# Scores of the rotary cross-attention: plain fp32 products, or three rounded products of high and low parts

## The chip, the cores and the metric

The kernel runs on one core of a Trainium2 chip. Its metric is the device time of one execution in microseconds (us); lower is better. Engines are called by their names in the profile: PE is TensorE (PEld its loads of the stationary operand), DVE is VectorE, ACT is ScalarE, POOL is GpSimd, SP issues the transfers.

## The reference

Six residual blocks on x (2 batches, 128 tokens, 512 wide). The change lies in the first, a cross-attention of 16 heads of 64 over a context of 2 x 2048 rows:

```python
lat = layer_norm(latents, ln_lat_g, ln_lat_b)          # 2 x 128 x 512
ctx = layer_norm(context, ln_ctx_g, ln_ctx_b)          # 2 x 2048 x 512
q = (lat @ Wq).reshape(b, n, HEADS, DHEAD).transpose(0, 2, 1, 3)
k, v = jnp.split(ctx @ Wkv, 2, axis=-1)                # 16 heads of 64
k = apply_rope(k, cos[None, None], sin[None, None])    # rotary, keys only
attn = jnp.einsum('bhnd,bhsd->bhns', q, k) * DHEAD ** (-0.5)
attn = jax.nn.softmax(jnp.clip(attn, -11.0, 11.0), axis=-1)
out = jnp.einsum('bhns,bhsd->bhnd', attn, v)
return out.transpose(0, 2, 1, 3).reshape(b, n, INNER) @ Wo + bo
```

Behind it come a causal self-attention, a product with the signs of a weight, a second cross-attention, a second causal self-attention and a mixture of experts. Everything is fp32.

## The kernel before

The first stage is `cross_attention_rotary`. The 4096 context rows are worked on in 8 chunks of 512 (`NC = 8`), four to a batch; the 16 heads in 4 groups of 4. A round t (`NT = 32`) is one chunk n = t // 4 with one group g = t % 4. A head's 64 components are two halves of 32 (the rotary pairs), and the four heads of a group lie on the four row groups of 32 partitions.

The engines run their own instruction streams in the written order and meet at semaphores. In a round:

- PE: in even rounds `values(v)` (L618, the value projection of half a chunk, four banks of `u_ps`) and `transposes` (L598) of half the next chunk; then `project(t)` (L633, the keys of chunk and group into the two banks of `k_ps`), `scores(t - 1)` (L648), `weigh(t - 2)` (L672). Projections are `split_matmul` (L55 to L59): each operand is split into a high part, rounded to the type fp32r, and a low part, the rounded rest; the product is high x high + high x low + low x high, each one matmul on rounded operands.
- `scores` is not split: for each of 4 column blocks j, 2 halves a and 4 heads i there is one plain fp32 product (L667) of a stationary 32 x 128 block of `turned` (rotated keys) with 128 columns of `q_T` (queries), and head i goes to bank i of `u_ps`.
- DVE: `turn(t)` (L331) rotates the keys out of `k_ps` into `turned` with six operations of 512 columns; `clip(t - 1)` (L354); and for chunk n + 2, spread over the rounds g = 1, 2 and 3, `stats`, `spread` and `center` (its layer norm, in place in `ctx_raw`). In round 18 it also takes two long reciprocals (L413), in round 19 it normalises the first batch (L419), in round 28 it adds the output bias.
- ACT: in even rounds `values` (copies of the values) and `context` (two writes a transposed quarter, one full, one rounded); `exponent(t - 1)`; `root`, the square root for a chunk's layer norm, in round g = 2.
- POOL: `split` makes the context's low part; `add_up(t - 1)` sums the probabilities, behind `clip`.
- SP: context (`ctx_raw`) and rotary tables (`tabs`) have two buffers each and are loaded a chunk or more ahead; then the output weights and those of the next stage.

The lowest 64 KB of the placed memory (`place`) hold the split weights of values and keys; the next stage's weights are loaded over them. The waits around the change, in `scores` and in `project`:

```python
pe.wait_ge(s["rope"], 6 * t + 6)                     # scores(t): rotation of round t complete
pe.wait_ge(s["exped"], 4 * t)                        # and the exponentials of round t - 1
...
pe.wait_ge(s["rope"], 6 * (t - 1) + 2 * a + 2)       # project(t): bank a of k_ps has been read
```

Of the kernel before, what the change touches and what calls it, by code (L numbers as in the profile page):

```python
# [16 lines left out]
ALU = mybir.AluOpType  # L17
# [139 lines left out]
def cross_attention_rotary(nc, I, env):  # L157
# [12 lines left out]
    with ExitStack() as st:  # L170
        names = ("vecs_in", "wq_in0", "wq_in1", "ctx_in0", "ctx_in1", "tab_in0", "tab_in1",
# [3 lines left out]
                 "wv_hi", "wv_lo", "wk_hi", "wk_lo", "v_mm", "v_out", "k_mm", "rope", "score", "exped", "clipped",  # L175
# [3 lines left out]
        s_ctx = [s["ctx_in0"], s["ctx_in1"]]  # L179
        s_tab = [s["tab_in0"], s["tab_in1"]]  # L180
# [16 lines left out]
        den = sb_in(st, "den", [P, 2, 512])  # L197
        bo = sb_in(st, "bo", [P, D])
# [17 lines left out]
        wo = ctx_raw[:].rearrange("p a c d -> p (a c) d")  # L216
# [11 lines left out]
        def _(sp):  # L228
            def load_ctx(n):
                if n >= 2:  # L230
                    sp.wait_ge(s["ctp"], 4 * (n - 1))
                sp.dma_start(ctx_raw[:, n % 2, :, :], I["ctx_rows"][n * 512:(n + 1) * 512, :]
                             .rearrange("(c p) d -> p c d", p=P)).then_inc(s_ctx[n % 2], 16)

            def load_tab(n):
                if n >= 2:
                    sp.wait_ge(s["rope"], 24 * (n - 1))
                c = n % 4
                sp.dma_start(tabs[:, n % 2, :, :], I["rot_tabs"][c * P:(c + 1) * P, :]
                             .rearrange("p (a n) -> p a n", a=2)).then_inc(s_tab[n % 2], 16)  # L240
# [21 lines left out]
            load_ctx(1)  # L262
# [5 lines left out]
            load_tab(1)  # L268
            load_wk(2)
            load_wk(3)  # L270
            load_ctx(2)
            for n in range(2, NC):
                if n + 1 < NC:
                    load_ctx(n + 1)
                load_tab(n)
                if n == 3:
                    sp.dma_start(env["causal"][:], I["causal4"]).then_inc(env["small_in"], 16)
                    for name, t in env["mo_small"].items():
                        sp.dma_start(t[:], I[name]).then_inc(env["small_in"], 16)
            rows4 = lambda n: I[n].rearrange("(k p) n -> p k n", p=P)  # L280
            sp.dma_start(bo[:], I["bo0"]).then_inc(s["bo_in"], 16)
            sp.wait_ge(s["ctp"], 4 * NC)
            sp.dma_start(wo, rows4("wo0")).then_inc(s["wo_in"], 16)
# [8 lines left out]
        def stats(dve, n):  # L292

            dve.wait_ge(s_ctx[n % 2], 16 * (n // 2 + 1))
            for c in range(4):
                dve.bn_stats(cst[:, c, :], ctx_raw[:, n % 2, c, :]).then_inc(s["c_step"], 1)
# [8 lines left out]
        def center(dve, n):  # L305
# [3 lines left out]
            for c in range(4):  # L309
                dve.tensor_scalar(ctx_raw[:, n % 2, c, :], ctx_raw[:, n % 2, c, :], cmv[:, n % 2, c, 0:1],  # L310
                                  crs[:, n % 2, c:c + 1], ALU.subtract, ALU.mult).then_inc(s["c_step"], 1)
# [6 lines left out]
        def _(dve):  # L318
# [12 lines left out]
            def turn(t):  # L331

                n, r = t // 4, t % 2
                cos, sin = tabs[:, n % 2, 0, :], tabs[:, n % 2, 1, :]
                if t % 4 == 0:
                    dve.wait_ge(s_tab[n % 2], 16 * (n // 2 + 1))
# [6 lines left out]
                if t >= 1:  # L343
# [8 lines left out]
                                  ALU.add).then_inc(s["rope"], 1)  # L352

# [26 lines left out]
            center(dve, 0)  # L380
            low_v(0)
            low_v(1)
            stats(dve, 1)
# [6 lines left out]
            for t in range(NT + 1):  # L390
                n, g = t // 4, t % 4
                if t < NT:
                    turn(t)
                if t >= 1:
                    clip(t - 1)
                if t == 1:
                    low_k(2)
                    low_k(3)
                if t < NT and 2 <= n + 2 < NC:
                    if g == 1:  # L400
                        stats(dve, n + 2)
# [8 lines left out]
                if t == 18:  # L410
                    dve.wait_ge(s["den_out"], 2)
                    for u in range(2):
                        dve.reciprocal(den[:, u, :], den[:, u, :]).then_inc(s["recip"], 1)  # L413
                if t == 19:
                    for u in range(2):
# [3 lines left out]
                        dve.tensor_tensor(half, half, den[:, u, :].rearrange("p (a t) -> p a t", a=4),  # L419
                                          ALU.mult).then_inc(s["normalised"], 1)  # L420
            for k in range(8):
# [4 lines left out]
                dve.reciprocal(den[:, k // 4, cols], u_ps[:, 2 + k // 4, cols]).then_inc(s["recip"], 1)  # L426
                dve.wait_ge(s["recip"], 2 + k + 1)
                dve.tensor_tensor(attn_T[:, k, P:2 * P], o_ps[:, k // 4, cols], den[:, k // 4, cols],
# [18 lines left out]
        def _(act):  # L447
# [1616 lines left out]
```

## Time and profile before

| | |
|---|---|
| time, median of 3 runs | 1193.22 us (1191.4 to 1197.19) |
| the profiled execution's own time | 1196.15 us |
| its span, first to last instruction | 1194.4 us |
| mean granted TensorE clock | 0.994 |
| TensorE busy | 1174.4 us, 98% |
| VectorE / ScalarE / GpSimd busy | 688.8 / 540.1 / 217.0 us |

The rotary stage ends some 541 us into the span; its 32 bursts of scores lie between 50.3 and 520.4. A row of the profile names engine, line, operation, the tile written and those read. "32\*128 32x128" is the stationary shape, then the moving one. A "busy" sum counts overlapping instructions once, so a mean duration times a count can be far more than it. Durations of matmuls include their way through the array; what one costs a stream is the distance between starts. A time in brackets at the end of a row is idle time before it, and what ended it.

### The profile page before, as it was taken

The page shows a single profiled execution, that of the slowest core. Times are in us where ns is not written, and L with a number is a line of the kernel's source. Part 1 is how long each engine was busy: PE and PEld are TensorE (multiplying, and loading weights), DVE is VectorE, ACT ScalarE, POOL GpSimd, SP SyncE. Part 2 cuts the span into 40 slices and gives each one's busy share as a digit, 9 for nine tenths or more (in the row PEclk, how much of TensorE's full clock was granted, in tenths as well). Part 3 has the DMA queues.
Part 4 walks back from the last instruction along what each step waited for, and adds up shares of the span by engine and source line. Part 5 has one row for each costly group of instructions (what it writes and reads, how often), then busy time and mean ns, then how long its engine had stood idle before and what let it go on. Part 6 is the DMA issues. An engine that isn't in the chain of part 4 may idle for free.

```text
span 1194.4 us, 23415 instructions
## 1 busy us (share of the span) xinstructions
PE 1174.4 (98%) x9888; PEld 963.8 (81%) x9888; DVE 688.8 (58%) x1220; ACT 540.1 (45%) x907; POOL 217.0 (18%) x178
## 2 busy tenths in 40 slices
PE   8999999999999999999899999999999999999998
PEld 6888888888788888864546667888899999999997
DVE  4654554545464533466788885265765566566562
ACT  4433324332433322224359997373644544444441
POOL 2243343444333443350000000010000000000000
PEclk9999999999999999999989999999999999999999
DMA  8210201010100020245232324301545445445440
GB/s 302 71 55 1 66 2 52 4 36 19 36 19 2 27 72 1 83 139 212 96 152 79 136 108 178 142 1 72 228 159 211 161 192 211 157 195 207 158 162 19
DMA packets 28160, 126.06 MB, mean 106 GB/s; under 512 B 2715, under 2 KB 2971, under 8 KB 17572
## 3 DMA queue, kind: packets, MB, share of 16 engines
q1 hardware_dynamic: 28068, 124.74, 27.9%
q8 instruction: 69, 1.13, 0.4%
q14 instruction: 23, 0.19, 0.0%
HBM read 124.20 MB, written 0.52 MB: 104 GB/s over the span
## 4 chain that ended last, share of the span: by engine, by line
PE 49%; issue 2%; DVE 2%; ACT 2%; DVEq 0%
PE mid_bk L57 11%; PE mid_bk L58 10%; PE mid_bk L59 10%; PE mid_bk L1105 5%; PE mid_bk L1120 2%; PE mid_bk L1150 2%; PE mid_bk L1076 2%; PE mid_bk L995 2%; PE mid_bk L1140 1%; PE mid_bk L1249 0%; ACT sa_sc L1415 0%; PE mid_bk L1201 0%; PE mid_bk L1190 0%; PE mid_bk L1050 0%; PE mid_bk L986 0%
## 5 line engine op out<-in xcount | busy, mean ns | idle before, releaser
L565 POOL TENSOR_TENSOR norm_both<-norm_both,prob 128x512 f32<-128x512 f32 x118 | 155.4, 1317 | 145.6 <-DVE prob L357 138.2
L494 ACT ACTIVATE prob<-u_ps 128x512 f32<-128x512 f32 x128 | 66.2, 605 | 181.5 <-PE u_ps L667 181.5
L57 PE MATMUL mid_bk<-mo_x_hi,mo_w_hi 128*128 128x256 f32 x496 | 141.0, 284 | 0.0
L58 PE MATMUL mid_bk<-mo_x_lo,mo_w_hi 128*128 128x256 f32 x496 | 141.0, 284 | 0.0
L59 PE MATMUL mid_bk<-mo_x_hi,mo_w_lo 128*128 128x256 f32 x496 | 141.0, 284 | 0.0
L340 DVE TENSOR_TENSOR turned<-k_ps,tabs 128x512 f32<-128x512 f32 x32 | 22.1, 690 | 189.7 <-PE k_ps L59 189.6
L1788 DVE TENSOR_TENSOR mo_w_lo<-w_raw,mo_w_hi 128x2048 fp32r<-128x2048 f32 x32 | 73.3, 2292 | 72.7 <-ACT mo_w_hi L1497 72.7
L57 PE MATMUL k_ps<-ctx_hi,wk_hi 128*128 128x512 f32 x256 | 102.8, 402 | 0.0
L57 PE MATMUL u_ps<-wv_hi,ctx_hi 128*128 128x512 f32 x256 | 101.7, 397 | 0.8 <-ACT prob L494 0.8
L483 ACT ACTIVATE vals<-u_ps 128x512 f32<-128x512 f32 x64 | 38.3, 598 | 141.2 <-PE u_ps L59 141.1
L1497 ACT ACTIVATE mo_w_hi<-w_raw 128x2048 fp32r<-128x2048 f32 x32 | 61.2, 1913 | 87.9 <-PE mid_bk L59 87.9
L57 PE MATMUL mid_bk<-mo_w_hi,mo_h_hi 128*128 128x512 f32 x256 | 100.2, 391 | 0.0
L58 PE MATMUL k_ps<-ctx_lo,wk_hi 128*128 128x512 f32 x256 | 100.2, 391 | 0.0
L58 PE MATMUL u_ps<-wv_lo,ctx_hi 128*128 128x512 f32 x256 | 100.1, 391 | 0.0
L58 PE MATMUL mid_bk<-mo_w_lo,mo_h_hi 128*128 128x512 f32 x256 | 100.0, 391 | 0.0
L59 PE MATMUL u_ps<-wv_hi,ctx_lo 128*128 128x512 f32 x256 | 99.7, 389 | 0.0
L59 PE MATMUL k_ps<-ctx_hi,wk_lo 128*128 128x512 f32 x256 | 99.7, 389 | 0.0
L59 PE MATMUL mid_bk<-mo_w_hi,mo_h_lo 128*128 128x512 f32 x256 | 99.6, 389 | 0.0
L58 PEld LDWEIGHTS mid_bk<-mo_x_lo,mo_w_hi 128*128 128x128 f32 x496 | 95.9, 193 | 1.2
L57 PEld LDWEIGHTS mid_bk<-mo_x_hi,mo_w_hi 128*128 128x128 f32 x496 | 95.8, 193 | 1.2
L59 PEld LDWEIGHTS mid_bk<-mo_x_hi,mo_w_lo 128*128 128x128 f32 x496 | 95.8, 193 | 0.0
L1505 ACT ACTIVATE mo_hid<-mid_bk,mo_b_cur 128x256 f32<-128x256 f32 x128 | 53.7, 472 | 86.8 <-PE mid_bk L59 86.7
(264 smaller groups left out, 2357.2 us busy)
## 6 DMA issues: line engine op xcount, KB each, us to landing
w_raw<-in_w SPq DMA_DIRECT2D x64, 1024.0 KB, 6.3
ctx_raw<-in_ctx_rows SPq DMA_DIRECT2D x8, 1024.0 KB, 5.5
x_k<-in_ctx_T SPq DMA_DIRECT2D x8, 1024.0 KB, 7.0
x_val<-in_ctx_heads SPq DMA_DIRECT2D x8, 1024.0 KB, 5.0
tabs<-in_rot_tabs SPq DMA_DIRECT2D x8, 512.0 KB, 3.8
vals<-in_wq_rows SPq DMA_DIRECT2D x4, 512.0 KB, 7.6
ctx_raw<-in_wo SPq DMA_DIRECT2D x1, 2048.0 KB, 9.7
x_mask<-in_mask SPq DMA_DIRECT2D x2, 1024.0 KB, 9.0
```

The costliest lines, as they stand in the source:

```text
L57: pe.matmul(out, w_hi, x_hi, start=start, stop=False)
L58: pe.matmul(out, w_hi, x_lo, start=False, stop=False)
L59: return pe.matmul(out, w_lo, x_hi, start=False, stop=stop)
L483: act.activation(vals[:, i, hv * 512:(hv + 1) * 512], u_ps[:, i, :], ACT.Copy).then_inc(s["v_out"], 1)
L494: act.activation(prob[:, t % 2, i, :], u_ps[:, i, :], ACT.Exp).then_inc(s["exped"], 1)
L565: ins = pool.tensor_tensor(to, to, src, ALU.add)
L995: ins = pe.matmul(bk[b][:, m, :], normed_T[:, k, b * P:(b + 1) * P], (wq, wk, wv)[m][:, k, :], start=(m == 2 and k == 0), stop=(k == KD - 1))
L1076: pe.matmul(s_ps[:, a, :], normed_T[rows, g, b * P:(b + 1) * P], k_raw[rows, n % 2, c * 512:(c + 1) * 512], start=True, stop=True).then_in ...
L1105: ins = pe.transpose(turned_at(q, a)[:, k * P:(k + 1) * P], x_sc[:, n % 2, a, (4 * c + k) * P:(4 * c + k + 1) * P], ident[:])
L1497: act.activation(w2_hi[:, r, :, :], w2_raw[:, r, :, :], ACT.Copy).then_inc(mo["w2_hi"], 1)
L1505: act.activation(hid[:, r, n, :], h_ps[:, 2 * r + n // 2, (n % 2) * TOK:(n % 2 + 1) * TOK], ACT.Gelu_apprx_tanh, bias=b1_cur[:, r, n:n + 1 ...
L1788: dve.tensor_tensor(w2_lo[:, r, :, :], w2_raw[:, r, :, :], w2_hi[:, r, :, :], ALU.subtract).then_inc(mo["w2_lo"], 1)
```

## The change

The scores become three rounded products like those of `split_matmul`: rounded keys `t_hi` with rounded queries `q_hi`, `t_hi` with the queries' low part `q_lo`, the keys' low part `t_lo` with `q_hi`. For it ACT rounds the rotated keys in every round (`high_turned`, behind the exponentials of the round before) and DVE subtracts (`low_turned`, behind `clip`); queries are rounded by ACT and their low part taken by DVE. `t_lo` lies over `turned`, `q_lo` under `den`. To make room, context and tables have one buffer in place of two, the bias lies in `causal` until that is loaded, the output weights are in two halves, and the next stage's weights `wp` are loaded in the next block. `center` moves from round g = 3 to the head of the next chunk's first round, `stats`, `spread` and `root` to round g = 3; the bias is added in round 13 and not 28.

```diff
@@ tiles and names
-        slabs = sb_in(st, "slabs", [P, 64 * 256 + (env["floor"] - env["base"]) // 4])
+        turned, den = place("turned", [P, 2, 2, 512], 64), place("den", [P, 8, TOK], 72)
+        t_lo, q_lo = place("t_lo", [P, 2, 2, 512], 64, F32R), place("q_lo", [P, NQ, 2, TOK], 72, F32R)
+        slabs = sb_in(st, "slabs", [P, 80 * 256 + (env["floor"] - env["base"]) // 4])
...
-        ctx_raw = sb_in(st, "ctx_raw", [P, 2, 4, D])
+        ctx_raw = sb_in(st, "ctx_raw", [P, 4, D])
-        tabs = sb_in(st, "tabs", [P, 2, 2, 512])
+        tabs = sb_in(st, "tabs", [P, 2, 512])
-        q_T = sb_in(st, "q_T", [P, NQ, 2, TOK])
-        turned = sb_in(st, "turned", [P, 2, 2, 512])
+        q_hi = sb_in(st, "q_hi", [P, NQ, 2, TOK], F32R)
+        t_hi = sb_in(st, "t_hi", [P, 2, 2, 512], F32R)
...
-        bo = sb_in(st, "bo", [P, D])
+        bo = env["causal"]
...
+        wo_half = ctx_raw, place("wo_second", [P, 4, D], 24)
@@ SP
             def load_ctx(n):
-                if n >= 2:
-                    sp.wait_ge(s["ctp"], 4 * (n - 1))
+                if n >= 1:
+                    sp.wait_ge(s["ctp"], 4 * n)
...
             def load_tab(n):
-                if n >= 2:
-                    sp.wait_ge(s["rope"], 24 * (n - 1))
+                if n >= 1:
+                    sp.wait_ge(s["rope"], 24 * n)
...
             load_wv(1)
-            load_ctx(1)
             load_wk(0)
             load_tab(0)
             load_wk(1)
             load_wv(2)
             load_wv(3)
-            load_tab(1)
+            load_ctx(1)
             load_wk(2)
             load_wk(3)
...
+            for n in range(NC):
+                if n >= 1:
+                    load_tab(n)
+                if n + 2 < NC:
+                    load_ctx(n + 2)
+                if n == 1:
+                    sp.dma_start(bo[:], I["bo0"]).then_inc(s["bo_in"], 16)
...
+                if n == 5:
+                    sp.wait_ge(s["bo_added"], NB)
+                    sp.dma_start(env["causal"][:], I["causal4"]).then_inc(env["small_in"], 16)
             sp.wait_ge(s["ctp"], 4 * NC)
...
             sp.wait_ge(s["v_mm"], 4 * 2 * NC)
-            for n, w in env["sa0_w"].items():
-                sp.dma_start(w[:], rows4("sa0_" + n)).then_inc(env["sa0_w_in"], 16)
+            sp.dma_start(wo_half[1][:], I["wo0"][512:1024, :].rearrange("(k p) n -> p k n", p=P)).then_inc(s["wo_in"], 16)
+            for n in ("wq", "wk", "wv"):
+                sp.dma_start(env["sa0_w"][n][:], rows4("sa0_" + n)).then_inc(env["sa0_w_in"], 16)
@@ DVE
+            def low_turned(t):
+                dve.wait_ge(s["t_hi"], t + 1)
+                dve.tensor_tensor(t_lo[:, t % 2, :, :], turned[:, t % 2, :, :], t_hi[:, t % 2, :, :],
+                                  ALU.subtract).then_inc(s["t_lo"], 1)
+
+            def low_queries(g):
+                dve.wait_ge(s["q_hi"], g + 1)
+                dve.scalar_tensor_tensor(q_lo[:, g, :, :], k_ps[:, g % 2, :].rearrange("p (a t) -> p a t", a=2), 0.125,
+                                         q_hi[:, g, :, :], ALU.mult, ALU.subtract).then_inc(s["q_out"], 1)
...
             center(dve, 0)
+            low_queries(0)
+            low_queries(1)
             low_v(0)
             low_v(1)
+            low_queries(2)
+            low_queries(3)
             stats(dve, 1)
...
             for t in range(NT + 1):
                 n, g = t // 4, t % 4
+                if 1 <= n and n + 1 < NC and g == 0:
+                    center(dve, n + 1)
                 if t < NT:
                     turn(t)
                 if t >= 1:
                     clip(t - 1)
+                if t < NT:
+                    low_turned(t)
...
-                if t < NT and 2 <= n + 2 < NC:
-                    if g == 1:
-                        stats(dve, n + 2)
-                    elif g == 2:
-                        spread(dve, n + 2)
-                    elif g == 3:
-                        center(dve, n + 2)
-                if t == 28:
+                if n + 2 < NC and g == 3:
+                    stats(dve, n + 2)
+                    spread(dve, n + 2)
+                if t == 13:
                     dve.wait_ge(s["bo_in"], 16)
@@ ACT
             def queries(g):
                 act.wait_ge(s["q_mm"], g + 1)
-                act.activation(q_T[:, g, :, :], k_ps[:, g % 2, :].rearrange("p (a t) -> p a t", a=2), ACT.Copy,
-                               scale=0.125).then_inc(s["q_out"], 1)
+                act.activation(q_hi[:, g, :, :], k_ps[:, g % 2, :].rearrange("p (a t) -> p a t", a=2), ACT.Copy,
+                               scale=0.125).then_inc(s["q_hi"], 1)
+
+            def high_turned(t):
+                act.wait_ge(s["rope"], 6 * t + 6)
+                act.activation(t_hi[:, t % 2, :, :], turned[:, t % 2, :, :], ACT.Copy).then_inc(s["t_hi"], 1)
...
                 if t >= 1:
                     exponent(t - 1)
-                if t < NT and n + 2 < NC and g == 2:
+                if t < NT:
+                    high_turned(t)
+                if t < NT and n + 2 < NC and g == 3:
                     root(act, n + 2)
@@ PE
             def scores(t):
...
-                pe.wait_ge(s["rope"], 6 * t + 6)
+                pe.wait_ge(s["t_lo"], t + 1)
...
                 for j in range(4):
                     cols = slice(j * P, (j + 1) * P)
-                    for a in range(2):
+                    for a, m in ((0, 0), (0, 1), (0, 2), (1, 0), (1, 1), (1, 2)):
+                        part_t, part_q = ((t_hi, q_hi), (t_hi, q_lo), (t_lo, q_hi))[m]
                         for i in range(4):
                             rows = slice(32 * i, 32 * i + 32)
-                            ins = pe.matmul(u_ps[:, i, cols], turned[rows, t % 2, a, cols],
-                                            q_T[rows, g, a, b * P:(b + 1) * P], start=(a == 0), stop=(a == 1))
+                            ins = pe.matmul(u_ps[:, i, cols], part_t[rows, t % 2, a, cols],
+                                            part_q[rows, g, a, b * P:(b + 1) * P], start=(a == 0 and m == 0),
+                                            stop=(a == 1 and m == 2))
...
-            pe.wait_ge(s["wo_in"], 16)
+            pe.wait_ge(s["wo_in"], 32)
@@ next stage
+            sp.dma_start(wp[:], rows("sa0_wp")).then_inc(sa0_w_in, 16)
             for n in range(2):
                 load_keys(n)
...
             def project_values(b):
+                pe.wait_ge(sa0_w_in, 16 * 10)
...
-            dve.wait_ge(sa0_w_in, 16 * 10)
             moments(1, 1)
```

## Rows read from the trace of the kernel before

**Rows 1.** The page, busy us, share of the span and instructions.
```profile
PE 1174.4 (98%) x9888; PEld 963.8 (81%) x9888; DVE 688.8 (58%) x1220; ACT 540.1 (45%) x907; POOL 217.0 (18%) x178
```
**Rows 2.** Busy time (instructions) by stretch: PE, PEld, DVE, ACT, POOL; clock, DMA.
```profile
210.00:270.00 60.00, 60.00 (x585) 50.21 (x585) 29.78 (x52) 21.13 (x35) 24.77 (x19) 1.00 0.08 20
```
**Rows 3.** Order of time around a burst of scores: start, duration, instructions.
```profile
256.31 1.88 PEld L667 LDWEIGHTS u_ps<-q_T,turned 32*128 32x128 f32 x64 [0.35 <-issue]
258.31 1.97 PE L683 MATMUL o_ps<-prob,vals 128*64 128x128 f32 x32
...
260.20 0.19 PEld L57 LDWEIGHTS k_ps<-ctx_hi,wk_hi 128*128 128x128 f32 x1 [0.17 <-issue]
260.31 0.19 PEld L58 LDWEIGHTS k_ps<-ctx_lo,wk_hi 128*128 128x128 f32 x1
```
**Rows 4.** Groups by line in the stage: count, busy us, mean ns, idle before.
```profile
L667 PEld LDWEIGHTS u_ps<-q_T,turned 32*128 32x128 f32 x2048 | 60.1, 186 | 11.5 <-issue 11.5
L58 PEld LDWEIGHTS k_ps<-ctx_lo,wk_hi 128*128 128x128 f32 x256 | 48.1, 188 | 9.1
...
L322 DVE TENSOR_TENSOR wv_lo<-prob,wv_hi 128x1024 fp32r<-128x1024 f32 x2 | 2.4, 1222 | 9.1 <-ACT wv_hi L451 9.1
...
L451 ACT ACTIVATE wv_hi<-attn_T 128x1024 fp32r<-128x1024 f32 x2 | 2.0, 1044 | 0.0
```
**Rows 5.** Order of time, loads of the experts' routing product.
```profile
829.67 0.97 PEld L1262 LDWEIGHTS mid_bk<-mo_wr,norm_both 128*128 128x128 f32 x8
```
**Rows 6.** Order of time, rounded products of 512 and of 256 columns.
```profile
1003.90 0.39 PE L59 MATMUL mid_bk<-mo_w_hi,mo_h_lo 128*128 128x512 f32 x1
1004.13 0.28 PE L57 MATMUL mid_bk<-mo_x_hi,mo_w_hi 128*128 128x256 f32 x1
...
1004.48 0.28 PE L57 MATMUL mid_bk<-mo_x_hi,mo_w_hi 128*128 128x256 f32 x1
```
**Rows 7.** Order of time, the second half of a chunk, all engines.
```profile
177.52 2.47 DVE L296 BATCH_NORM_STATS2 cst<-ctx_raw 128x6 f32<-128x512 f32 x4
...
199.30 1.08 DVE L303 TENSOR_SCALAR cva<-cmv 128x4 f32<-128x4 f32 x1
...
203.96 2.07 PE L667 MATMUL u_ps<-q_T,turned 32*128 32x128 f32 x64
...
206.05 2.07 ACT L494 ACTIVATE prob<-u_ps 128x512 f32<-128x512 f32 x4 [4.13 <-PE u_ps L667]
...
206.68 1.90 DVE L357 TENSOR_SCALAR prob<-prob 128x512 f32<-128x512 f32 x4
...
208.65 5.60 POOL L565 TENSOR_TENSOR norm_both<-norm_both,prob 128x512 f32<-128x512 f32 x4 [4.20 <-DVE prob L357]
...
208.70 5.84 DVE L310 TENSOR_SCALAR ctx_raw<-ctx_raw,cmv,crs 128x512 f32<-128x512 f32 x4
...
218.92 1.03 PE L602 MATMUL u_ps<-ident,ctx_raw 128*128 128x128 f32 x8
```
**Rows 8.** Order of time, the last burst of the stage.
```profile
518.30 2.07 PE L667 MATMUL u_ps<-q_T,turned 32*128 32x128 f32 x64 [0.33 <-ACT prob L494]
```
**Rows 9.** Order of time, VectorE in round 18.
```profile
325.57 6.55 DVE L413 RECIPROCAL den<-den 128x512 f32<-128x512 f32 x2
```
**Rows 10.** Order of time, the start of the stage.
```profile
31.14 1.92 DVE L310 TENSOR_SCALAR ctx_raw<-ctx_raw,cmv,crs 128x512 f32<-128x512 f32 x4
...
38.40 1.03 PE L602 MATMUL u_ps<-ident,ctx_raw 128*128 128x128 f32 x8
...
46.73 0.69 DVE L351 TENSOR_TENSOR turned<-turned,part 128x512 f32<-128x512 f32 x1
...
50.26 2.07 PE L667 MATMUL u_ps<-q_T,turned 32*128 32x128 f32 x64
```
**Rows 11.** The page, transfers: KB of one, us to landing.
```profile
ctx_raw<-in_ctx_rows SPq DMA_DIRECT2D x8, 1024.0 KB, 5.5
...
tabs<-in_rot_tabs SPq DMA_DIRECT2D x8, 512.0 KB, 3.8
```

More of the change, by code:

```diff
@@ L215, in cross_attention_rotary @@
         summed = norm_both[:].rearrange("p a n -> p (a n)").rearrange("p (h t) -> p h t", h=H)
-        wo = ctx_raw[:].rearrange("p a c d -> p (a c) d")
+        den = den[:, :, 0:P]
+        wo_half = ctx_raw, place("wo_second", [P, 4, D], 24)
+        wo = lambda k: wo_half[k // 4][:, k % 4, :]
         prob_raw = prob[:].rearrange("p a i n -> p (a i n)")
@@ L267, in _ @@
             load_wv(3)
-            load_tab(1)
+            load_ctx(1)
             load_wk(2)
             load_wk(3)
[L271 to L277, printed above, removed]
+            rows4 = lambda n: I[n].rearrange("(k p) n -> p k n", p=P)
+            for n in range(NC):
[5 more added lines that the diff above has]
+                    sp.dma_start(bo[:], I["bo0"]).then_inc(s["bo_in"], 16)
                     for name, t in env["mo_small"].items():
                         sp.dma_start(t[:], I[name]).then_inc(env["small_in"], 16)
-            rows4 = lambda n: I[n].rearrange("(k p) n -> p k n", p=P)
-            sp.dma_start(bo[:], I["bo0"]).then_inc(s["bo_in"], 16)
+                if n == 5:
+                    sp.wait_ge(s["bo_added"], NB)
+                    sp.dma_start(env["causal"][:], I["causal4"]).then_inc(env["small_in"], 16)
             sp.wait_ge(s["ctp"], 4 * NC)
-            sp.dma_start(wo, rows4("wo0")).then_inc(s["wo_in"], 16)
+            sp.dma_start(wo_half[0][:], I["wo0"][0:512, :].rearrange("(k p) n -> p k n", p=P)).then_inc(s["wo_in"], 16)
             sp.wait_ge(s["v_mm"], 4 * 2 * NC)
-            for n, w in env["sa0_w"].items():
-                sp.dma_start(w[:], rows4("sa0_" + n)).then_inc(env["sa0_w_in"], 16)
+            sp.dma_start(wo_half[1][:], I["wo0"][512:1024, :].rearrange("(k p) n -> p k n", p=P)).then_inc(s["wo_in"], 16)
+            for n in ("wq", "wk", "wv"):
+                sp.dma_start(env["sa0_w"][n][:], rows4("sa0_" + n)).then_inc(env["sa0_w_in"], 16)
             sp.wait_ge(s["k_mm"], 2 * NT)
@@ L333, in turn @@
                 n, r = t // 4, t % 2
-                cos, sin = tabs[:, n % 2, 0, :], tabs[:, n % 2, 1, :]
+                cos, sin = tabs[:, 0, :], tabs[:, 1, :]
                 if t % 4 == 0:
-                    dve.wait_ge(s_tab[n % 2], 16 * (n // 2 + 1))
+                    dve.wait_ge(s["tab_in"], 16 * (n + 1))
                 if t >= 2:
@@ L412, in _ @@
                     for u in range(2):
-                        dve.reciprocal(den[:, u, :], den[:, u, :]).then_inc(s["recip"], 1)
+                        half = den[:, 4 * u:4 * u + 4, :]
+                        dve.reciprocal(half, half).then_inc(s["recip"], 1)
                 if t == 19:
@@ L418, in _ @@
                         half = attn_T[:, 4 * u:4 * u + 4, 0:P]
-                        dve.tensor_tensor(half, half, den[:, u, :].rearrange("p (a t) -> p a t", a=4),
-                                          ALU.mult).then_inc(s["normalised"], 1)
+                        dve.tensor_tensor(half, half, den[:, 4 * u:4 * u + 4, :], ALU.mult).then_inc(s["normalised"], 1)
             for k in range(8):
@@ L709, in project_out @@
                     pe.wait_ge(s["normalised"], 2 + k + 1 if b else k // 4 + 1)
-                    ins = pe.matmul(k_ps[:, b, :], attn_T[:, k, b * P:(b + 1) * P], wo[:, k, :],
+                    ins = pe.matmul(k_ps[:, b, :], attn_T[:, k, b * P:(b + 1) * P], wo(k),
                                     start=(k == 0), stop=(k == 7))
```

34 lines of the change are left out of this document (16 added, 18 removed).

## The prediction

> **What bounds the kernel now.** I read the page's busy shares first, then the busy times by stretch, then the order of time in one round of the loop. TensorE is busy 98% of the span, the next engine 58% [rows 1]. The share is an average, so the rotary stage has to be read by itself: in the stretch shown, and in each like it from 90 to 510, TensorE is busy for 60.00 of 60.00 us at a granted clock of 1.00, while VectorE works 29.78, ScalarE 21.13, GpSimd 24.77 [rows 2]. There every microsecond that TensorE gets more or less moves the end, and the other engines count only where they make it wait. One burst of scores runs from 256.31 until the weighing starts at 258.31: 2.00 us for 64 instruction pairs, 32 bursts in all, 2048 pairs [rows 3, 4]. The loop writes 4 x 2 x 4 = 32 products, so a plain fp32 product is two pairs (load and matmul), and four of them, one for each row group, run side by side: the loads last 1.88 us with 0.19 for the last one, so the 16 foursomes follow one another every (1.88 - 0.19) / 15 = 0.113 us.
>
> **The scores, on the path.** A burst now has 4 blocks x 2 halves x 3 products x 4 row groups = 96 products in place of 32. A rounded product is one pair: the loop of the keys writes 256 for each of its three lines and 256 are recorded [rows 4]. So 64 pairs become 96, 16 foursomes 24. The question is what sets the pace of a foursome, the load or the streaming of 128 columns.
> - The load. Eight products with a moving operand of only 8 columns have loads that take 0.97 us together, so (0.97 - 0.19) / 7 = 0.111 us apart [rows 5]: with next to nothing to stream, a load of 128 columns still costs 0.11. A rounded operand's load is no shorter, 188 ns against 186 of the scores, and at the start of a projection the second rounded load follows the first after 260.31 - 260.20 = 0.11 us [rows 3, 4]. The change keeps all 128 stationary columns. Also two products that share a stationary operand load it twice (L57 and L58 do), so the shared rounded keys save none.
> - The streaming. No rounded product of this trace has fewer than 256 columns. One of 512 columns takes 1004.13 - 1003.90 = 0.23 of TensorE, three of 256 take 0.35 or 0.12 each [rows 6], so 0.11 for 256 columns more and, in proportion, 0.12 - 0.055 = 0.065 for 128: below the load. The upper bound is the plain product of two pairs, 2 x 0.113 = 0.226.
> I take 0.113 for a foursome, the load, since that row has the same 32 x 128 stationary shape. The sum: 8 more foursomes x 0.113 = 0.90 us a burst, x 32 bursts = +28.9 us. From 0.108 to 0.125 (a full burst's mean, 2.00 / 16) it would be +25.0 to +38.0 (24 times the pace less 1.81, times 32).
>
> **The rounding, beside the path.** ScalarE gets one copy of 128x1024 in a round (1.05 us, as the rounding of the values' weights [rows 4]), VectorE one subtraction of that size (1.22). VectorE works half of the time [rows 2], so 1.22 in a round of some 15.5 is carried. What counts is where they stand. With S the start of a burst in round t, the rotation of round t has ended before the exponentials of t - 1 do; these start at S + 2.1 and the clip at S + 2.8 now [rows 7], 0.9 later with the longer burst; ScalarE has the copy behind its exponentials and ends it at S + 6.1, VectorE its subtraction behind the clip and ends at S + 7.4. The scores of round t come only behind the weighing (S + 4.9) and the next projection (5.7 us more): S + 10.5, so 3 us are left. Three places have no such projection, or more in front:
> - The last round. Behind the last projection come scores(30), weigh(29) and at once scores(31), which now start 0.33 us after TensorE is free, behind the exponentials (518.30) [rows 8]. Then they wait for the low part: S + 7.4 against S + 4.9, 2.5 us, less the 0.33: +2.2 us. Behind this wait stand weigh(30), the output projection and the next stage.
> - Rounds 18 and 19. VectorE's two long reciprocals (6.55 us) [rows 9] come behind the low part of round 18 and push the rotation of 19, its clip, its low part, and now also the statistics and the centering of the context chunk, which stand behind all of them. Counting from the values of round 18: reciprocals to 33.5, rotation 37.2, clip 39.1, low part 40.4, statistics and spread 44.4, square root, the normalising pair 45.7, centering 48.0; the transposes want it at 45.8. +2.2 us, once.
> - The change of chunk, six times. The statistics moved from the second round of a chunk to its last, the centering from there to the round behind, ahead of its rotation. With S in the last round: low part S + 7.4, four statistics (2.47) 9.9, aggregate 10.3, variance (1.08) 11.3, root 11.6, centering from 12.0. The transposes want it when the values are through, at S + 15.9 (now 218.92 - 203.96 = 15.0, plus 0.9). Centering has taken 5.84 us beside four additions of GpSimd and 1.92 alone [rows 7, 10]; the additions run from S + 5.6 to 11.0, so I take 1.92, done at S + 14.0: nothing, with 1.9 us in hand. ScalarE waits in its root too, with the copies of the values behind it; TensorE asks for those only at the transposes.
>
> **The rest, at nothing.** Start: q_out is now raised by VectorE, behind ScalarE's rounding; four subtractions of some 0.7 us, the last of them behind the last query product, push the second chunk's centering back by some 3.6 us, from its end at 33.1 to 36.7; the transposes come at 38.40 [rows 10]. If the cover goes it costs what is late, under 1 us. The burst of round 0 starts at 50.26; its rotation ends at 47.4, so the low part is there at 47.4 + 1.1 + 1.2 = 49.7 [rows 10]. Context and tables now have one buffer each: the next chunk's load waits for the second pair of transposes and takes 5.5 us [rows 11], wanted over 15 us later; a table (3.8 us) is loaded behind the last rotation of its chunk and wanted 17 us later. On SP's queue each stands in the order in which it is released; the bias, asked for in round 13, is issued in round 6. The second half of the output weights waits for the last values and has one round, some 20 us, for 5. The projection weights moved to the next stage put 1 MB ahead of the keys on that queue: some 5 us of transfers; the weights are wanted only behind the next attention's weighing, the keys behind the whole of it. I price them from 0 to +2.
>
> **Sum.** 28.9 + 2.2 + 2.2 = +33.3 on the profiled execution's own 1196.15 us. That execution was 2.9 above the median of the runs, 1193.22, so the forecast is 1193.2 + 33.3 = 1226.5. Its own range is 1218 to 1236 (25.0 with no stall; 38.0 with 4.4).
>
> **Rivals.**
> - Faster: a rounded load is hidden and the stream sets the pace. At 0.065 a foursome 24 take 1.56 us against 1.81 now, -0.25 x 32 = -8; at 0.053, half of the increment for 256 columns without any overhead, -17. With the stalls, +4.4, it is 1181 to 1190; it is decided below 0.070. Against it stand the rows of 188 ns and of 0.11 us between loads. The Trainium skill's page "TensorE: Matmul & The Clock Gate", section "Weight-path perf modes — Fast Weight Load (FWL) and DoubleRow", says that fast loading is on when 128 weights are loaded and their type is not FP32; if the rounded type fell under it, the load would be short and this rival right. The trace disagrees so far, 188 ns rounded and 186 plain [rows 4]. Chance 0.07.
> - A narrow rounded product streams no faster than a plain one: 0.226 a foursome, 24 x 0.226 - 1.81 = 3.61 a burst, +115.6, with the last round's wait +118: 1311. For it: the trace has none under 256 columns, so nothing excludes it. Against: 256 and 512 are in proportion. Chance 0.11. That the row groups don't run side by side at all (96 x 0.111 = 10.7 a burst, +278) gets 0.02.
> - The change of chunk is late. If the centering meets GpSimd's additions it takes 5.84, ends at S + 17.9 and TensorE waits 2.0 us six times: +12, 1238. The Trainium skill's page "SBUF — State Buffer", section "Who interferes with whom", says that a VectorE instruction with two SBUF inputs contends with a GpSimd instruction that reads SBUF; by it the new subtraction, which starts with the additions, could wait for one of them, 1.3 us more, in the last round and in the chain of the chunk. The trace has something of it: 5.84 against 1.92 for the centering. Chance 0.12.
>
> **How the numbers follow.** Forecast 0.68, late chunk 0.12, slow narrow product 0.11, hidden load 0.07, serial 0.02. The range 1214 to 1246 holds the first two, 0.80. A measurement of this kernel tells 0.5% from no change: faster needs under 1187.3, within reaches to 1199.2. The hidden load gives the first two thirds of the time: faster 0.05, same 0.03, slower 0.92.
>
> **What would show it.** Right: the loads of a burst 23 x 0.113 + 0.19 = 2.8 us long, 96 of them, 3072 in all; bursts of 2.9 us; TensorE idle before scores(31) for 2.5 us and before the transposes of round 20 only. It would be wrong if the loads of a burst stood clearly under or over 0.11 apart, or if the transposes waited at each change of chunk.

## The result, and the profile after

The changed kernel takes 1229.38 us (median of 4 runs, 1225.54 to 1229.48), the kernel before 1195.2 us beside it (4 runs, 1191.4 to 1197.31). The ratio is 1.029, 95% interval 1.0269 to 1.0311, so the change makes the kernel slower by 34.2 us. The profiled executions have spans of 1227.5 and 1194.4 us; this difference, 33.1, is what the rows below have to account for.

The page after (busy us, share, instructions), against [rows 1]: TensorE has 1024 instructions more, the 32 more of each of 32 bursts, and its share is the same 98%.
```profile
PE 1203.5 (98%) x10912; PEld 995.0 (81%) x10912; DVE 728.1 (59%) x1256; ACT 568.4 (46%) x939; POOL 241.8 (20%) x178
```
The same dense stretch after, against [rows 2] (PE, PEld, DVE, ACT, POOL, then clock and DMA). TensorE is still busy for all 60 us at full clock; VectorE has 34.49 in place of 29.78 and is far from its limit.
```profile
210.00:270.00 60.00, 60.00 (x686) 51.00 (x686) 34.49 (x55) 22.40 (x36) 26.75 (x19) 1.00 0.09 28
```
The loads of one burst of scores in order of time (start, duration), against the load row of [rows 3]. The operands change with each foursome, so each has its own row. From 211.57 to 214.14 there are 23 steps, 2.57 us: 0.112 us each, whichever parts are multiplied. The weighing follows at 214.40: 2.83 us for the burst where it was 2.00.
```profile
211.57 0.19 PEld L692 LDWEIGHTS u_ps<-q_hi,t_hi 32*128 32x128 f32 x4 [0.35 <-issue]
211.68 0.19 PEld L692 LDWEIGHTS u_ps<-q_lo,t_hi 32*128 32x128 f32 x4
211.79 0.20 PEld L692 LDWEIGHTS u_ps<-q_hi,t_lo 32*128 32x128 f32 x4
...
214.14 0.20 PEld L692 LDWEIGHTS u_ps<-q_hi,t_lo 32*128 32x128 f32 x4
214.40 1.73 PEld L709 LDWEIGHTS o_ps<-prob,vals 128*64 128x64 f32 x32
```
TensorE's waits from 0 to 560 us (us in total, times, longest). Two are new: 3.1 us on the low part of the turned keys, once, and 1.1 us on the centering, once. The six changes of chunk don't stand there.
```profile
PE u_ps L692 <- DVE t_lo L359: 3.1, 1, 3.1
...
PE u_ps L626 <- DVE ctx_raw L313: 1.1, 1, 1.1
```
The last round of the stage on TensorE, against [rows 8]: after the weighing of chunk 29 it waits 3.14 us, then the burst begins at the usual 0.11 a foursome, and from 547.57 on each takes 0.21. The burst lasts 552.20 - 547.13 = 5.07 us and the weighing behind it 2.96.
```profile
542.03 1.97 PE L709 MATMUL o_ps<-prob,vals 128*64 128x128 f32 x32
547.13 0.33 PE L692 MATMUL u_ps<-q_hi,t_hi 32*128 32x128 f32 x4 [3.14 <-DVE t_lo L359]
547.30 0.28 PE L692 MATMUL u_ps<-q_lo,t_hi 32*128 32x128 f32 x4
547.41 0.38 PE L692 MATMUL u_ps<-q_hi,t_lo 32*128 32x128 f32 x4
547.57 0.43 PE L692 MATMUL u_ps<-q_hi,t_hi 32*128 32x128 f32 x4
547.78 0.43 PE L692 MATMUL u_ps<-q_lo,t_hi 32*128 32x128 f32 x4
...
552.20 2.96 PE L709 MATMUL o_ps<-prob,vals 128*64 128x128 f32 x32
555.09 3.70 PE L736 MATMUL k_ps<-ctx_raw,attn_T 128*128 128x512 f32 x8
```
The same place by stretch (the column behind POOL's count is the granted clock): TensorE did nothing for 3.1 us, and behind that its granted clock is 0.53, which is the lower of its two levels, 1.2 GHz, for nearly all of 7.2 us.
```profile
544.00:547.10 3.10, 0.00 (x0) 0.00 (x0) 2.50 (x3) 1.13 (x2) 2.29 (x2) 1.00 0.97 355
547.10:554.30 7.20, 7.17 (x116) 7.05 (x118) 1.26 (x3) 2.02 (x4) 3.66 (x3) 0.53 0.06 23
```
**The account of the profiled pair.** The span from the weighing of chunk 29 to the first output projection is a ruler that needs no other part of the trace: 522.19 - 516.00 = 6.19 us before, 555.09 - 542.03 = 13.06 after, +6.87. Of it 0.83 is the longer burst, 2.81 the wait (3.14 less 0.33), and 3.23 is burst and weighing at the lower clock (5.07 - 2.83, and 2.89 - 1.90 from start to start). The rows of before for it:
```profile
516.00 1.97 PE L683 MATMUL o_ps<-prob,vals 128*64 128x128 f32 x32
...
520.30 1.97 PE L683 MATMUL o_ps<-prob,vals 128*64 128x128 f32 x32
522.19 1.12 PE L710 MATMUL k_ps<-ctx_raw,attn_T 128*128 128x512 f32 x2
```
Over the stage: 32 bursts x 0.83 = +26.6, the last wait +2.8, the clock behind it +3.2, the wait in round 20 +1.1, and a start that is 0.6 us earlier. That is +33.1 against 555.09 - 522.19 = +32.9 measured. The earlier start is not the change's doing: the first transposes begin at 38.40 us before, at 37.80 here, and at 38.48 in a second profile of the changed kernel (changed_again below). Behind the stage nothing more is lost: both executions have falls of the clock there, 13.6 and 13.7 us in sum at the lower level.

### The profile page after: what moved, and what is told of

Its sections match the earlier page's. It is cut to its first block, busy times and chain, and to the rows that moved or that the text cites. A ratio compares the mean times of both kernels' runs of the same rounds, so it can differ in the third digit from the quotient of the medians.

```text
span 1227.5 us, 25534 instructions
## 1 busy us (share of the span) xinstructions
PE 1203.5 (98%) x10912; PEld 995.0 (81%) x10912; DVE 728.1 (59%) x1256; ACT 568.4 (46%) x939; POOL 241.8 (20%) x178
## 4 chain that ended last, share of the span: by engine, by line
PE 47%; DVE 2%; issue 2%; ACT 1%; DVEq 0%
PE mid_bk L57 10%; PE mid_bk L58 10%; PE mid_bk L59 10%; PE mid_bk L1133 4%; PE mid_bk L1178 2%; PE mid_bk L1148 2%; PE mid_bk L1104 2%; PE mid_bk L1022 2%; PE mid_bk L1168 1%; PE mid_bk L1277 0%; ACT sa_sc L1443 0%; DVE x_sc L1724 0%; PE mid_bk L1229 0%; PE mid_bk L1218 0%; PE mid_bk L1078 0%
## 5 line engine op out<-in xcount | busy, mean ns | idle before, releaser
L589 POOL TENSOR_TENSOR norm_both<-norm_both,prob 128x512 f32<-128x512 f32 x118 | 180.2, 1527 | 156.6 <-DVE prob L370 149.2
L1533 ACT ACTIVATE mo_hid<-mid_bk,mo_b_cur 128x256 f32<-128x256 f32 x128 | 53.6, 471 | 86.7 <-PE mid_bk L59 86.7
L1724 DVE CUSTOM_DVE_ANT_0 x_sc<-mid_bk,x_mask 128x512 f32<-128x512 f32 x128 | 80.9, 687 | 4.6 <-issue 4.6
```

Source lines behind the costliest of these rows:

```text
L589: ins = pool.tensor_tensor(to, to, src, ALU.add)
L1533: act.activation(hid[:, r, n, :], h_ps[:, 2 * r + n // 2, (n % 2) * TOK:(n % 2 + 1) * TOK], ACT.Gelu_apprx_tanh, bias=b1_cur[:, r, n:n + 1 ...
L1724: dve.tensor_tensor_reduce(x_sc[:, n % 2, a, cols], s_ps[:, a, :], mask[:, b, cols], 1.0, -3.0e38, ALU.add, ALU.max, x_tops[:, n % 2, a, c ...
```

## The experiments

Nine kernels ran. The first four and the next four each ran together beside the kernel before (medians 1193.2 and 1192.49 us), the last alone (1192.12). "First output projection" is the start of that line in a profile; the kernel before has it at 522.19 us, the changed one at 555.09. The theory: a foursome (the four products that run side by side, one for each row group) costs what its stationary load costs, 0.11 us for 128 columns, and the rest of the loss sits in the two waits and what they set off. The rivals: the matmul or its streaming sets the pace, or the frame (one buffer each, the moved order) costs much more than its waits.

**narrow_moving.** The two products with a low part move 64 columns in place of 128. In this and the next edits the stop flag and the signal at the end of the burst move to the product that is now last (not shown). The scores of half the queries so lack the correction.
```
-  for a, m in ((0, 0), (0, 1), (0, 2), (1, 0), (1, 1), (1, 2)):
+  for a, m in ((0, 0), (0, 1), (0, 2), (1, 1), (1, 2), (1, 0)):
+      w = P if m == 0 else P // 2
...
-          ins = pe.matmul(u_ps[:, i, cols], part_t[rows, t % 2, a, cols], part_q[rows, g, a, b * P:(b + 1) * P], ...)
+          ins = pe.matmul(u_ps[:, i, j * P:j * P + w], part_t[rows, t % 2, a, cols], part_q[rows, g, a, b * P:b * P + w], ...)
```


> Leaves out half of the query columns in four of the six products of each block (high x low and low x high, but for the last product, which keeps all 128): 16 of the 24 foursomes of a burst have a moving operand of 64 columns instead of 128; the loads of the stationary operand stay at 128 columns. Load theory: the loads set the pace, so nothing moves: foursomes 0.112 us apart, a burst 2.8 us to the weighing, the time within 1 us of the changed kernel's. Stream theory (a rounded product of 128 columns streams at half the rate of a wide one, 0.107 us, and the load is covered): 16 x 0.053 = 0.85 us less a burst, 2.0 us, 27 us less in all.

Measured: 1231.55 us (1229.24 to 1233.86, 2 runs), ratio 1.0319 [1.0289, 1.0349]. Foursomes with 64 moving columns start 0.11 us apart as before (402.56, 402.67), and the burst is 405.14 - 402.31 = 2.83 us, as with 128 columns:
```profile
402.31 0.33 PE L693 MATMUL u_ps<-q_hi,t_hi 32*128 32x128 f32 x4
402.48 0.25 PE L693 MATMUL u_ps<-q_lo,t_hi 32*128 32x64 f32 x4
402.56 0.28 PE L693 MATMUL u_ps<-q_hi,t_lo 32*128 32x64 f32 x4
402.67 0.28 PE L693 MATMUL u_ps<-q_lo,t_hi 32*128 32x64 f32 x4
...
405.14 3.51 PE L710 MATMUL o_ps<-prob,vals 128*64 128x128 f32 x32
```
The streaming doesn't set the pace. The clock of this kernel, and the long weighing in the last row, are taken up in the last section.

**short_load.** The mirror of it: the stationary operand of the same sixteen foursomes has 64 columns, the moving one 128. The scores of half the keys so lack the correction.
```
-  for a, m in ((0, 0), (0, 1), (0, 2), (1, 0), (1, 1), (1, 2)):
+  for a, m in ((0, 0), (0, 1), (0, 2), (1, 1), (1, 2), (1, 0)):
+      w = P if m == 0 else P // 2
...
-          ins = pe.matmul(u_ps[:, i, cols], part_t[rows, t % 2, a, cols], ...)
+          ins = pe.matmul(u_ps[0:w, i, cols], part_t[rows, t % 2, a, j * P:j * P + w], ...)
```


> The counterpart: in the same 16 foursomes of a burst the stationary operand has 64 columns instead of 128 and the moving one keeps its 128, so half of the key rows get no low-part products. Load theory: the 16 shorter loads cost about 0.055 to 0.065 us instead of 0.112, a burst takes 8 x 0.112 + 16 x 0.06 + 0.15 = 2.0 us, about 27 us less in all than the changed kernel. Stream theory: nothing moves, 2.8 us.

Measured: 1202.3 us (1198.83 to 1203.61, 3 runs), ratio 1.0067 [1.0045, 1.009]. The loads of a burst: behind a foursome of 128 columns the next starts 0.11 us later, behind one of 64 only 0.06, and 24 foursomes take 258.44 - 256.44 = 2.00 us. In a row of loads the second shape is that of the loaded, stationary operand; the products of the 64-column loads still move 128 columns.
```profile
256.44 0.19 PEld L693 LDWEIGHTS u_ps<-q_hi,t_hi 32*128 32x128 f32 x4 [0.35 <-issue]
256.55 0.14 PEld L693 LDWEIGHTS u_ps<-q_lo,t_hi 32*64 32x64 f32 x4
256.61 0.14 PEld L693 LDWEIGHTS u_ps<-q_hi,t_lo 32*64 32x64 f32 x4
...
258.44 1.73 PEld L710 LDWEIGHTS o_ps<-prob,vals 128*64 128x64 f32 x32
```
The two kernels have the same count of products and of instructions. Halving what is loaded takes 0.83 us out of a burst, halving what is streamed takes nothing: the load sets the pace. Fewer stationary columns also mean fewer rows of output, which this edit alone doesn't separate from the load; the routing product of [rows 5], with 8 moving columns and loads 0.111 us apart, speaks for the load. Since here 128 columns stream within 0.06, a load that took no time would have made the changed burst shorter than before (an estimate: 24 x 0.06 + 0.26 = 1.70 us). So the rival of the hidden load had its price about right and its condition wrong.

**plain_in_new_frame.** Everything of the change but the products: the parts are read as plain fp32 and multiplied by the two plain products of before (high parts only).
```
-  for a, m in ((0, 0), (0, 1), (0, 2), (1, 0), (1, 1), (1, 2)):
+  for a in range(2):
-          ins = pe.matmul(u_ps[:, i, cols], part_t[rows, t % 2, a, cols], part_q[rows, g, a, b * P:(b + 1) * P], ...)
+          ins = pe.matmul(u_ps[:, i, cols], t_hi[rows, t % 2, a, cols].bitcast(F32), q_hi[rows, g, a, b * P:(b + 1) * P].bitcast(F32), ...)
```


> Everything of the change but its products: buffers, order, rounding on ScalarE, subtraction on VectorE and all waits stay, the scores are again 32 plain fp32 products a burst, of the rounded keys with the rounded queries (the low parts are computed and not used). Mine: bursts of 2.0 us as before; what is left is the frame: the wait before scores(31) of about 3 us, half the clock behind it (3 us more), about 1 to 2 us before the transposes of round 20, less 0.6 at the start: 5 to 8 us above the kernel before, 1200 to 1203. Rival, that the frame costs nothing and the whole difference is the products: within 1 us of the kernel before. Rival, that the frame is the larger part: over 15 us above.

Measured: 1202.48 us (1199.64 to 1206.12, 6 runs), ratio 1.0074 [1.0052, 1.0095]: +9.3 us by the medians, a little over the 5 to 8 expected. The burst is 2.00 us again, the first output projection 529.75, +7.56. Its waits, from the list of TensorE's waits, and the last burst and weighing:
```profile
PE u_ps L691 <- DVE t_lo L359: 3.1, 1, 3.1
...
PE u_ps L626 <- DVE ctx_raw L313: 1.9, 1, 1.9
```
```profile
523.06 3.80 PE L691 MATMUL u_ps<-q_hi,t_hi 32*128 32x128 f32 x64 [3.12 <-DVE t_lo L359]
526.79 3.03 PE L707 MATMUL o_ps<-prob,vals 128*64 128x128 f32 x32
```
There are 2.8 us more in the last round, 1.9 in round 20, and 2.8 at the lower clock behind the last wait (burst 3.73 in place of 2.00, weighing 2.96 in place of 1.90 from start to start) make 7.5 of the 7.56. So the frame costs its two waits and the clock, and the other moves (single buffers, the later centering, the queue) cost nothing that shows. With shorter bursts the wait of round 20 is 1.9 and with the changed ones 1.1: the 0.83 us more of each burst cover part of it.

**two_products.** The product with the low part of the turned keys is left out: sixteen foursomes.
```
-  for a, m in ((0, 0), (0, 1), (0, 2), (1, 0), (1, 1), (1, 2)):
+  for a, m in ((0, 0), (0, 1), (1, 0), (1, 1)):
```


> Leaves out the product of the keys' low part with the rounded queries: 16 foursomes a burst instead of 24. Load theory: 2.83 - 8 x 0.112 = 1.94 us a burst, so 28 to 29 us less than the changed kernel, 1200 to 1202, still above the kernel before for the frame's waits. If a rounded foursome cost more at the start or end of a burst than inside, the burst would end clearly above 1.94.

Measured: 1201.55 us (1199.31 to 1202.78, 4 runs), ratio 1.0064 [1.0042, 1.0086], first output projection 526.55; burst 516.00 - 514.06 = 1.94 us. Sixteen rounded foursomes cost what sixteen of plain products do, less 0.06. A plain fp32 product here is just two loads of 128 columns, and three rounded ones are three.

**changed_again, fill_last_wait, weigh_first, weigh_first_late_recip.** The second set takes the last round apart. changed_again is the changed kernel once more.

> The changed kernel once more, beside the next three on the same chip. 33 to 35 us above the kernel before; 3 to 4 us less in a run in which the clock does not fall behind the wait of the last round.

Measured: 1226.87 us (1226.16 to 1230.44, 5 runs), ratio 1.0293 [1.0276, 1.031]. The last round repeats: the wait 3.14, from weighing to output projection 555.07 - 542.76 = 12.31 us. The lower clock again lasts 6.8 us, but it begins later, so part of its cost falls on the output projection (4.47 us where the changed kernel has 3.70).

fill_last_wait gives TensorE three products of no use during the wait:
```
   if t == NT:
+      pe.wait_ge(s["rope"], 6 * NT)
+      for _ in range(3):
+          pe.matmul(k_ps[:, 1, :], part[:, 0, 0:P], part[:, 1, :], start=True, stop=True)
```


> The changed kernel with three plain products of 512 columns on data that nobody needs, into a bank of k_ps that is free, between weigh(29) and scores(31): TensorE has some 2.6 us of work in the wait of 3.1 us, the wait itself stays. If the fall of the clock behind that wait costs what it seems to (a burst of 5.07 us instead of 2.83 and a weighing of 2.9 instead of 1.97), the granted clock stays at 1.00 and the time falls by 3.2 us against changed_again. If the burst is slow for another reason (the transfers that run at 355 GB/s then, GpSimd beside it), nothing is gained.

Measured: 1224.37 us (1222.43 to 1227.37, 5 runs), ratio 1.0256 [1.0242, 1.027]. The last round in order of time and the stretch's clock:
```profile
544.32 1.97 PE L709 MATMUL o_ps<-prob,vals 128*64 128x128 f32 x32
546.22 2.84 PE L776 MATMUL k_ps<-part 128*128 128x512 f32 x6
549.43 0.33 PE L692 MATMUL u_ps<-q_hi,t_hi 32*128 32x128 f32 x4 [0.37 <-DVE t_lo L359]
...
552.26 1.97 PE L709 MATMUL o_ps<-prob,vals 128*64 128x128 f32 x32
554.16 3.70 PE L736 MATMUL k_ps<-ctx_raw,attn_T 128*128 128x512 f32 x8
```
```profile
549.00:558.00 9.00, 8.63 (x141) 6.14 (x142) 2.15 (x5) 3.35 (x5) 6.96 (x7) 1.00 0.16 60
```
By the ruler it is 554.16 - 544.32 = 9.84 us in place of 13.06: 3.2 less, though the scores start no earlier behind the weighing (549.43 - 544.32 = 5.11 us; 547.13 - 542.03 = 5.10 in the changed kernel). So the 3.2 us were the clock's, and it fell because TensorE had stood still: the other engines' work at this place is the same, and the transfers run here too (306 GB/s from 546.0 to 549.4 us). The profiles agree: a wait of 3.1 us stands in six of them (changed, changed_again and the first four experiments), and each has a fall behind it; the four with this wait filled or cut to 1.0 us or less (this one, the next two and one_product) have none there. By the medians the gain over changed_again is 2.5 us where 3.2 was expected.

weigh_first turns the last two steps round, so that a weighing lies in the wait:
```
+  if t == NT:
+      weigh(t - 2)
   if 1 <= t <= NT:
       scores(t - 1)
-  if t >= 2:
+  if 2 <= t < NT:
       weigh(t - 2)
```


> In the last round weigh(30) goes ahead of scores(31): it needs clip(30), which is done 2.4 us before the low part. Then the 2.0 us of weighing lie in the wait, which shrinks from 3.1 to about 0.7 + 0.5 us in two pieces, and the clock has no idle stretch of 3 us before it: 2 us of the wait and 3.2 us of the clock, so 5 us less than changed_again. If only the wait is gained, 2 us.

Measured: 1224.46 us (1220.68 to 1226.5, 5 runs), ratio 1.0269 [1.0253, 1.0285]. The waits of the last round are two of 0.7 and 0.5 us, the clock stays at 1.00, and the first output projection is at 550.26, 4.8 earlier than in the changed kernel (5 expected):
```profile
542.31 1.97 PE L709 MATMUL o_ps<-prob,vals 128*64 128x128 f32 x32
544.99 1.97 PE L709 MATMUL o_ps<-prob,vals 128*64 128x128 f32 x32 [0.71 <-DVE prob L370]
...
550.26 3.70 PE L736 MATMUL k_ps<-ctx_raw,attn_T 128*128 128x512 f32 x8
```
The ruler shows 7.95; two weighings and a burst need 1.90 + 1.90 + 2.83 = 6.63 of it. The medians give only 2.4 of the 4.8 back. The profiled execution was the lowest run, 1220.68, with a mean granted clock of 0.999 against 0.996 in changed_again; how often the clock falls in the stages behind differs from one execution to the next, and that scatter is as large as this gain. (In changed_again the fall of the last round, from 549.8 us on, is the only one from there to the end of the work; the profile of the changed kernel has 13.7 us more at the lower level behind the stage.) The fastest run of each kernel is the nearer comparison: changed_again 1226.16 us at a granted clock of 0.996, fill_last_wait 1222.43 at 0.999, weigh_first 1220.68 at 0.999, so 3.7 and 5.5 us less where 3.2 and 5 were expected.

weigh_first_late_recip also moves the two long reciprocals of [rows 9] and the normalising from rounds 18 and 19 to 21 and 22, away from the change of chunk.
```
-  if t == 18:
+  if t == 21:
       (the two reciprocals)
...
-  if t == 19:
+  if t == 22:
       (the normalising)
```


> As weigh_first, and VectorE's two long reciprocals and the normalising of the first batch move from rounds 18 and 19 to rounds 21 and 22, where VectorE has the time of a value projection before its next rotation. The wait of 1.1 us before the transposes of round 20 goes: 1 us less than weigh_first, 6 less than changed_again, and still 27 us above the kernel before, 32 x 0.83 for the bursts. If the wait there came from something else than the reciprocals, nothing changes.

Measured: 1223.55 us (1218.96 to 1225.18, 5 runs), ratio 1.0253 [1.0231, 1.0274]. The wait in round 20 is gone, the first output projection at 548.72, 1.5 earlier than in weigh_first. It still stands 26.5 us behind the kernel before, and 32 x 0.83 is 26.6. The last round still waits 0.7 and 0.5 us (0.33 before), and this execution's first transposes came 0.6 us earlier than before, which nearly cancels. So with the wait of 3.1 us, that of round 20 and the clock out of the way, the loss of the stage is the longer bursts. Moving waits doesn't give them back. By the medians this kernel is 3.3 us below changed_again, by the fastest runs 7.2; 6 were expected.

**one_product.** The theory's other end: eight foursomes, high parts only, in the order of weigh_first_late_recip.
```
-  for a, m in ((0, 0), (0, 1), (0, 2), (1, 0), (1, 1), (1, 2)):
+  for a, m in ((0, 0), (1, 0)):
...
-  if t < NT:
-      low_turned(t)                    (VectorE, each round)
...
-  pe.wait_ge(s["t_lo"], t + 1)
+  pe.wait_ge(s["t_hi"], t + 1)
```


> One product of high parts only, eight foursomes a burst: both products with a low part are left out (so the scores have the precision of the rounded high parts), the low part of the turned keys isn't computed, and the order of weigh_first_late_recip is kept. Load theory (a burst is so many foursomes at 0.112 us plus a fixed end): two_products had 1.94 us for 16 foursomes, so 1.94 - 8 x 0.112 = 1.04 us here, 0.96 less than the 2.00 of the kernel before, x 32 = -30.7 us; the waits are gone in this order, so first out projection at about 522.2 - 31 = 491.5 us and about 1193 - 31 = 1162 us (1159 to 1167), a ratio of about 0.974. Rival 1 (a burst has a floor of its own, not set by its count): burst 1.5 us, -16 us, 1177. Rival 2 (with a shorter round another engine ends later than TensorE, the centering or the exponentials): burst 1.04 but waits of TensorE on VectorE or ScalarE of 0.3 us or more a round, 1172 or more.

Measured: 1166.04 us (1163.2 to 1166.45, 5 runs), ratio 0.976 [0.9737, 0.9783], 26.1 us faster than the kernel before. In the trace the burst is 304.44 - 303.40 = 1.04 us, and the first output projection starts at 491.37 where 491.5 was expected.
```profile
303.40 0.97 PEld L690 LDWEIGHTS u_ps<-q_hi,t_hi 32*128 32x128 f32 x32 [0.35 <-issue]
...
304.44 1.73 PEld L707 LDWEIGHTS o_ps<-prob,vals 128*64 128x64 f32 x32
```
No other engine became the bound: from 210 to 270 us TensorE is busy for all 60.00. The median lies 4 us over the 1162 expected, inside the range given; the span of 1164.4 keeps all but 0.8 of the stage's 30.8 us (1194.4 - 1164.4 = 30.0). It is faster than the kernel before because it computes less: its scores have the precision of the rounded high parts.

## Why the prediction was right

- **The scores, on the path: right, 0.83 a burst and not 0.90.** The pace was 0.112 against the 0.113 taken from [rows 3]. What was missed is the end of a burst: from the last foursome's load to the weighing it is 2.00 - 1.69 = 0.31 us with plain products and 214.40 - 214.14 = 0.26 with rounded ones. Together with the pace that makes 26.6 us of the forecast 28.9. narrow_moving, short_load, two_products and one_product all fit 0.112 for each foursome of 128 columns and 0.26 at the end: 15 x 0.112 + 0.26 = 1.94, 7 x 0.112 + 0.26 = 1.04.
- **The last round: the mechanism right, 2.8 and not 2.2.** The subtraction was taken at 1.22 us, as it had stood alone; here it takes 1.91.
```profile
545.16 1.91 DVE L359 TENSOR_TENSOR t_lo<-turned,t_hi 128x1024 fp32r<-128x1024 f32 x1 [0.51 <-ACT t_hi L496]
```
```profile
544.74 6.18 POOL L589 TENSOR_TENSOR norm_both<-norm_both,prob 128x512 f32<-128x512 f32 x4 [4.15 <-DVE prob L370]
```
  It lies inside GpSimd's four additions, as in most rounds: the median of its 32 durations is 1.95 us. The additions too are longer (1527 ns in the mean over the stage; 1317 without the change). In rounds 18 and 19, where it starts ahead of the first addition, it takes 1.24 and 1.21, and 1.22 in round 17 (315.36), where no addition runs. The Trainium skill's page "SBUF — State Buffer", section "Who interferes with whom", says that a VectorE instruction with two SBUF inputs contends with a GpSimd instruction that reads SBUF. The trace agrees, and the price here is 0.7 us, where the prediction's rival reckoned with 1.3; no run takes the additions away. The prediction had the contention as a rival's means and left it out of the sum.
- **Not predicted at all: the clock, +3.2.** The forecast treated a wait on TensorE as costing its own length. Behind this one the granted clock went to the lower level and a burst and a weighing took 3.2 us more; the wait's real price was 6.0. fill_last_wait shows it: the burst starts as long behind the weighing as here, but TensorE stands idle for only 0.37 us, and there is no fall.
- **Round 20: right in kind, 1.1 and not 2.2.** The chain came as described, with steps of other sizes. The forecast took the clip at 1.9 us, but its four operations last 411 to 428 ns each in every round and spread over 1.9 only where they follow the exponentials one by one. In round 19 these had ended (349.06), and the clip took 1.42 (350.80); the trace of before has the same 1.42 for that clip (335.58). The variance took 0.41 in place of 1.08. The normalising pair went the other way: 2.38 us (356.52) beside GpSimd's additions, where before it took 1.28 (342.19) behind them. The subtraction (1.21, from 352.14) was ahead of the round's first addition (353.91), as long as forecast.
- **The change of chunk: right.** The centering took 1.92 and no wait came (223.90, the statistics from 219.41, as the chain has it). The rival of a late chunk was nearer than the forecast had it: GpSimd's additions, begun at 217.11 and 6.28 us long, ended at 223.39, only 0.5 us ahead of the centering. The start: 0.6 us the other way, within what executions of one kernel differ by.

So the total (+33.3 against +33.1 in the profiled pair; +34.2 by the medians) is better than its parts: two terms too large by 2.3 and 1.1, one too small by 0.6, one of 3.2 missing, and 0.6 taken off again by the start. The forecast case was the one that happened; its closeness is partly luck.

## What to carry to other kernels

Count the loads, not the products: where small matmuls in row groups have 128 stationary columns, the load sets the pace, and splitting a plain fp32 product (two loads) into three rounded ones (three loads) costs half as much again, and with 64 moving columns as much as with 128. Put the smaller operand in the stationary place if one has to be small. And price a wait of some microseconds on a busy TensorE by the work behind it as well, since that can run at the lower clock. A weighing put into the gap took 5.1 us out of the last round (13.06 less 7.95 by the ruler), where the wait alone was 3.1.

## What the runs showed of the hardware that was not expected

- With 64 stationary columns foursomes started 0.06 us apart, with 128 columns 0.112, with 128 moving columns in both: the pace follows the stationary columns, nearly in proportion.
- The clock fell without any wait in narrow_moving. In the middle of the dense stage, with TensorE recorded busy throughout, it was at the lower level for 3.4 us twice, and the weighing there took 3.51 us in place of 1.97 (405.14, shown at narrow_moving):
```profile
395.00:405.40 10.40, 10.40 (x137) 8.89 (x137) 3.78 (x6) 3.44 (x6) 2.59 (x2) 1.00 0.34 128
405.40:408.80 3.40, 3.40 (x33) 3.07 (x30) 2.23 (x5) 2.85 (x5) 0.95 (x1) 0.50 0.00 0
```
  Read two microseconds at a time from 60 us to the last round, the other profiles of this study show no fall but one. So the narrow moving operands may be the reason; that is argued and not shown. The one other fall is of 3.4 us in short_load, and it stands behind its wait of 1.9 us in round 20; the same waits of plain_in_new_frame (1.9) and two_products (2.0) have none behind them. Ahead of 60 us, narrow_moving and fill_last_wait have one of 3.4 us each, from 53.6 and 53.8 us on; so fill_last_wait reaches its last weighing later (544.32) than the changed kernel (542.03), and only the ruler compares the two. It is also open why this kernel's ratio is 1.0319 and that of changed_again 1.0293; with 2 runs and intervals that overlap it may be nothing.
- The same wait of 3.1 us brought a fall of 6.8 us in the changed kernel, changed_again, short_load and plain_in_new_frame, of 10.2 us in narrow_moving and of 3.4 us in two_products, where it began 1.6 us into the burst. So falls behind the same wait differed in length by a factor of three.
